# Expert pass in another order, with the whole weights loaded in two steps and the last waits moved to SyncE

## The reference

```python
def reference(x, ...):
    xn = _layernorm(x)
    return x + attention(xn) + ffn(xn)

def attention(x):                       # causal linear attention with a gate
    xn = _layer_norm(x, ln_g, ln_b)
    q, k, v = split(xn @ qkv_w + qkv_b)
    k = elu(k * sigmoid(xn @ gate_w + gate_b)) + 1
    q = elu(q) + 1
    num = (tril(q @ k.T)) @ v
    den = sum(q * cumsum(k)) + 1e-6
    return num / den

def ffn(x):                             # eight experts, two per token
    gates = sinkhorn((x @ router_w.T + router_b) / temp)
    topk_vals, topk_idx = top_k(gates, 2)
    g, p = relu(x @ wg[e]), x @ wp[e]   # 128 -> 256
    all_out[e] = (g * p) @ wo[e]        # 256 -> 128
    return x + sum(all_out[topk_idx] * topk_gates)
```

## Time and profile before

| | us |
|---|---|
| median of 3 runs | 374.01 (373.85 to 376.59) |
| profiled execution, its own time | 375.94 |
| its span, first to last instruction | 373.90 |
| TensorE busy | 335.1 |
| GpSimd busy | 267.3 |
| VectorE busy | 268.1 |
| ScalarE busy | 235.6 |
| mean granted clock of TensorE | 0.978 |

### The profile page before, as it was taken

One profiled execution on the slowest core, in us unless ns is written; L12 is line 12 of the kernel. 1 busy time (PEld: TensorE's weight loads), 2 busy tenths in 40 slices (PEclk: granted clock), 3 DMA queues, 4 the chain that ended last, 5 costly groups with the idle time before them and its releaser, 6 DMA issues.

```text
span 373.9 us, 8933 instructions
## 1 busy us (share of the span) xinstructions
PE 335.1 (90%) x2584; PEld 304.9 (82%) x2584; DVE 268.1 (72%) x735; ACT 235.6 (63%) x442; POOL 267.3 (71%) x363
## 2 busy tenths in 40 slices
PE   0799899888999999988779999999999999999980
PEld 0789568656888888868779999999989999999980
DVE  3998889989888888785625667666666667666650
ACT  2689753225766766756525787777767777776540
POOL 3686999955777766657627767777777777777772
PEclk9999999989999999999969999999999999999996
DMA  6999999997434423248988887554565565564110
GB/s 179 285 327 334 337 332 276 319 258 231 145 108 142 144 100 118 84 127 232 310 270 259 254 228 200 176 161 129 154 188 158 163 163 164 142 185 114 58 35 0
DMA packets 64285, 70.97 MB, mean 190 GB/s; under 512 B 6098, under 2 KB 59102, under 8 KB 64240
## 3 DMA queue, kind: packets, MB, share of 16 engines
q1 hardware_dynamic: 54112, 48.70, 48.2%
q0 software_dynamic: 8672, 21.19, 15.7%
q10 hardware_dynamic: 1456, 0.53, 0.7%
HBM read 28.54 MB, written 43.04 MB: 191 GB/s over the span
## 4 chain that ended last, share of the span: by engine, by line
PE 69%; DVE 15%; DMA 6%; issue 4%; POOL 3%; ACT 2%; SPq 0%; POOLq 0%; ACTq 0%; DVEq 0%
PE psum L1712 16%; PE psum L1697 7%; PE psum L1699 7%; PE psum L1698 7%; PE psum L1687 5%; PE psum L1585 4%; PE psum L1521 4%; PE psum L1673 4%; PE psum L1414 3%; DVE stats L887 3%; DMA rows<-by_lower 2%; DMA rows<-in_L_attn_x 2%; POOL out L598 2%; PE psum L1467 2%; PE psum L1468 2%
## 5 line engine op out<-in xcount | busy, mean ns | idle before, releaser
L576 POOL DMA_INDIRECT by_lower<-rows,slot_u x64 | 63.9, 999 | 29.9 <-issue 18.5
L598 POOL DMA_INDIRECT out<-rows x70 | 68.8, 983 | 21.5 <-issue 16.2
L1712 PE MATMUL psum<-w_expert,hT 128*128 x560 | 77.5, 278 | 0.8 <-DVE hT L1347 0.5
L1697 PE MATMUL psum<-xT_high,w_now 128*128 128x256 f32 x232 | 70.4, 303 | 1.9 <-DVE xT_low L1338 1.2
L587 POOL DMA_INDIRECT by_upper<-rows x58 | 57.1, 985 | 20.3 <-issue 12.0
L1712 PEld LDWEIGHTS psum<-w_expert,hT 128*128 128x128 f32 x560 | 69.8, 193 | 1.5 <-issue 1.1
L799 ACT ACTIVATE w_now<-w_split 128x1024 fp32r x58 | 61.4, 1059 | 13.4 <-PE psum L1699 12.8
L1698 PE MATMUL psum<-xT_low,w_now 128*128 128x256 f32 x232 | 65.4, 282 | 0.0
L1699 PE MATMUL psum<-xT_high,w_now 128*128 128x256 f32 x232 | 65.3, 282 | 0.0
L1351 DVE TENSOR_TENSOR hT<-relu,psum 128x512 f32<-128x512 f32 x58 | 39.9, 687 | 33.7 <-ACT relu L818 17.1
L818 ACT ACTIVATE relu<-psum 128x512 f32<-128x512 f32 x58 | 34.6, 597 | 20.4 <-PE psum L1699 20.4
(11 more groups left out here) (271 smaller groups left out, 705.7 us busy)
## 6 DMA issues: line engine op xcount, KB each, us to landing
by_lower<-blank SPq DMA_DIRECT2D x1, 10140.0 KB, 35.3
by_upper<-blank SPq DMA_DIRECT2D x1, 10062.0 KB, 71.3
rows<-by_upper SPq DMA_DIRECT2D x29, 258.0 KB, 2.9
rows<-by_lower SPq DMA_DIRECT2D x23, 260.0 KB, 3.4
rows<-in_L_attn_x SPq DMA_DIRECT2D x8, 512.0 KB, 9.1
lead_row<-by_lower SPq DMA_DIRECT2D x6, 260.0 KB, 2.8
rows<-by_lower SPq DMA_DIRECT2D x12, 130.0 KB, 4.4
rows<-by_upper SPq DMA_DIRECT2D x12, 129.0 KB, 2.3
```

Of the source, the lines that this page charges most:

```text
L576: pool.indirect_dma_start(by_lower, bass.IndirectOffsetOnAxis(ap=slot_u[:, t:t + 1], axis=0), rows[:, t, :], None)\
L598: pool.indirect_dma_start(out_rows, bass.IndirectOffsetOnAxis(ap=row(n)[:, k, TOKEN:TOKEN + 1].bitcast(U32), axis=0), row(n)[:, k, BASE], ...
L1697: pe.matmul(target, high, x_high, start=True, stop=False)
L1712: last = pe.matmul(psum[:, 4 + n % 2, k * D:(k + 1) * D], hT[:, n % 3, f, k * P:(k + 1) * P], weights, start=(f == 0), stop=(f == FB - 1))
```

## The change

It has four parts. `FRONT` = 18 takes the place of `LEAD` as the number of long entries ahead of the twelve short ones, so the first pass is eighteen long, twelve short and eleven long entries; the lead buffers stay six. The floor of `need_first` becomes 18. The weights of `w_whole` are issued in two steps, the first ahead of the load of entry 10, the second ahead of entry 12, and the last expert's weights ahead of entry 20; the places where ScalarE and VectorE split them move along. And the waits for the last 18 `row_out` semaphores go from GpSimd to SyncE.

```diff
+    FRONT = 18
...
-    FIRST_PASS = [*range(LEAD), *range(PAIRS, NE), *range(LEAD, PAIRS)]
+    FIRST_PASS = [*range(FRONT), *range(PAIRS, NE), *range(FRONT, PAIRS)]
...
             for n in range(LEAD):
                 load_row(n, by_lower, ROW)
-            sp.wait_ge(o_chunk, G)
-            sp.dma_start(w_whole[:, :, 0:FF], wg.rearrange("e p f -> p e f")).then_inc(whole_loaded, 16)
-            sp.dma_start(w_whole[:, :, FF:2 * FF], wp.rearrange("e p f -> p e f")).then_inc(whole_loaded, 16)
             for n in range(LEAD, NE):
                 if n == LEAD + 4:
+                    sp.wait_ge(o_chunk, G)
+                    sp.dma_start(w_whole[:, :, 0:FF], wg.rearrange("e p f -> p e f")).then_inc(whole_loaded, 16)
+                if n == LEAD + 6:
+                    sp.dma_start(w_whole[:, :, FF:2 * FF], wp.rearrange("e p f -> p e f")).then_inc(whole_loaded, 16)
+                if n == FRONT + 2:
                     load_expert(E - 1)
                 load_row(n, by_lower, ROW)
             for n in range(NE, 2 * NE):
                 load_row(n, by_upper, ROW_UP)
+            for n in range(2 * NE - NB, 2 * NE):
+                sp.wait_ge(row_out[n % NB], gone_after(n))
...
-            for n in range(2 * NE - NB, 2 * NE):
-                pool.wait_ge(row_out[n % NB], gone_after(n))
...
-                    if a == 0 and i == LEAD + 14:
+                    if a == 0 and i == FRONT + 12:
                         round_expert(E - 1)
...
-                        if n + 4 == LEAD:
+                        if n + 4 == FRONT:
                             act.wait_ge(whole_loaded, 32)
...
-                step(dve.tensor_scalar(need_first[:], need[:], pair_end[:, 0:1], float(LEAD), ALU.add, ALU.max))
+                step(dve.tensor_scalar(need_first[:], need[:], pair_end[:, 0:1], float(FRONT), ALU.add, ALU.max))
...
-                    if a == 0 and i == LEAD + 15:
+                    if a == 0 and i == FRONT + 13:
                         divide_expert(E - 1)
```

## The result

| | before | after |
|---|---|---|
| median, timed in the same rounds | 376.55 (6 runs) | 370.01 (6 runs) |
| ratio after / before | | 0.984 (0.981 to 0.988) |
| profiled execution, its own time | 375.94 | 368.30 |
| its span | 373.90 | 365.50 |
| last scatter into by_lower to last scatter to out ("the stage") | 190.35 | 184.63 |

The changed kernel is 6.5 us faster by the medians and 5.9 by the ratio. Three of the six runs of before are those whose median was 374.01 ahead of the change. The forecast was 8.1 us faster and 365.9; the measured 370.0 lies above the range (364.4 to 369.0).

A forecast was written before the change was run, and what follows sets the result against it. It took TensorE to bound the kernel, with GpSimd almost as late; 6.8 us from the hole before entry 6 and 1.3 at the end, 8.1 off 374.01, gave 365.9 us, range 364.4 to 369.0.

The forecast's parts named there:

- The hole before entry 6: Start of the expert stage: TensorE's idling and slow clock, with entry 6's load behind the weights, cost 6.8 us, all regained.
- The landing of entry 6: After the last by_lower scatter: 3.4 us for the scatter, 3.4 for the load, landed at 183.0, 1.7 us early.
- No loss at entries 10 and 12: First pass, row loads behind the moved weights: between 6 us early and 2.8 us late, loss taken as nothing.
- rival B: First pass: entry 12 up to 2.8 us late, or GpSimd idling more; about 1.5 us back, 367.4; chance 0.17.
- The second pass and its later floor: Second pass: first load at about 248, 11 us later than before, at no cost, with 16 us of cover.
- GpSimd follows: Expert stage: GpSimd runs through the first pass to 268.9 and is 1.8 us early for the second.
- The end: End of program: with SyncE waiting for the last landings, GpSimd's DRAIN starts earlier; 1.3 us gained, between 0 and 2.3.
- rival A: End of program: GpSimd's DRAIN waits for the landing on its own, so only 6.8 us are won, 367.2; chance 0.20.
- The sum: Whole kernel: 6.8 us from the hole before entry 6 plus 1.3 at the end, 8.1 us in all.
- The absolute number: Whole kernel: 8.1 us taken from the median of 374.01, giving 365.9 us.

The follow-up runs named there:

- t_before: The kernel before, unchanged, run against itself to show the noise; ratio 0.996 (0.993 to 1.000).
- s_after: The changed kernel, unchanged, run once more beside other runs; 370.1 us, 0.983 of before.
- t_poolwaits: The changed kernel with the last eighteen waits back on GpSimd instead of SyncE; 0.987 of before.
- s_by_expert: The changed kernel with the whole weights in sixteen transfers of 128 KB, two ahead of each load of entries 8 to 15; 368.4 us, 0.981 of before.
- s_second_at_16: The changed kernel with the second half of the whole weights issued ahead of entry 16 instead of entry 12; 369.5 us, 0.983 of before.

## Why the prediction was right or wrong

Two terms of the forecast failed: the base of the sum, 374.01, which was 2.5 us too low, and the loss at entry 12, which was put at nothing and was 1.1 us. The mechanism at entry 6 and that at the end were right.

- **The hole before entry 6.** Right in cause and size: 6.8 us were put on it, and the stage without any hole is 6.5 to 6.8 us shorter than before's first profile (190.35 - 183.6 to 183.9). In the later profile of before (t_before) the stage was 191.6. TensorE lost 0.7 us more there (turn of entry 5 to turn of entry 8 in 14.5 us against 13.7) after much the same hole, 5.00 us: its granted clock was still 0.71 from 194 to 196, where it was 1.00 in the first profile. And GpSimd, waiting 1.63 and 1.45 us for landings in the short entries, never idled again before the second pass, so it was the later of the two. So the hole costs 6.5 to 8.0, and GpSimd's reserve in the old order was small. The stretch of t_before:

```profile
194.00:196.00 2.00, 2.00 (x15) 2.00 (x15) 0.81 (x3) 0.00 (x0) 0.72 (x1) 0.71 0.45 113
```

- **The landing of entry 6.** Mis-sized. The forecast had 3.4 for the scatter and 3.4 for the load, and 1.7 us to spare. The scatter took 3.82. The trace of after has no landing for entry 6's own load, but the next one took 4.6; with that it landed at 183.25 for a turn at 183.35, so nothing was to spare. In s_after it was 0.54 late. Of the lead loads the forecast had only 2.8; in later profiles their median was 3.4 to 4.3, in either order.
- **No loss at entries 10 and 12.** This is the step of the argument that failed; entry 10 was in time, entry 12 was not. The text set 283 KB per us (6 us early) against 168 (2.8 late) and took no loss. The measured rate from the issue of entry 6's load to the landing of entry 12's is 3868 KB / (199.61 - 178.65) = 185 KB per us, and 175 in s_after, close to the slow bound, which was itself a measured row. The fast one was no row at all: 0.92 us was SyncE's pace of issue for four loads of short entries, 130 KB each, and the text gave it 260 KB. The hole before entry 12 was 1.1 us in the profile of after, 1.5 and 0.2 in two others (s_after, t_poolwaits). It was named as rival B with a chance of 0.17; it should have been the forecast. The rule of the Trainium skill (DMA: Bandwidth & Descriptors, section "Queues, rings and completion order"), that descriptors are consumed in ring order on each DMA engine, stood beside it and pointed to this. The runs agree: in after the load behind the second 1024 KB took 12.3 us, in s_by_expert those with 256 KB of weights between them 4.3 to 5.9.
- **The second pass and its later floor.** Right: its first load went out at 246.4 (248 forecast), and TensorE did not idle on a row there.
- **GpSimd follows.** Right in that it was not the later one, and in part by luck. It did not run through the short entries: it lost 0.7 and 1.0 us there beyond its pause of 0.30, waiting for VectorE's rows. Of the 1.8 us forecast for the start of the second pass 0.9 were left (1.16 less the pause), and that with TensorE a hole later than forecast.
- **The end.** Right, 1.3 us of the span, by the mechanism that was taken: the DRAIN is 4.98 us of GpSimd's own time from the end of its last instruction. The DRAIN's row read 7.64 us, and a DRAIN that had grown was what the prediction had put down as the sign of rival A; that sign was badly chosen, since an earlier start alone lengthens it. In the other profiles with SyncE waiting it starts 0.2 to 2.3 us before the last scatter, reads 6.2 to 8.2 us, and ends 4.98 after that scatter's instruction each time. Rival A is out: the end did shrink.
- **The sum.** 8.1 forecast. In the stage and at the end 5.7 + 1.3 = 7.0; the missing 1.1 is the second hole. In device time 5.9 to 6.5: the rest, 0.5 to 1.1 us, is about what the new order has more around its span (2.8 to 4.2 us in the six executions of after, where the sum kept the 2.04 of before). The sum had no term for that, and its cause stays open.
- **The absolute number.** The larger part of the miss of 4.1 us is the base. The 8.1 were taken from 374.01, the median of three runs. In the rounds of after the median of before was 376.55, and 376.3 to 377.5 in the three other groups. The profiled run's own 375.94, which the text set aside, was the better base: it would have given 367.8. So 2.5 us of the miss are the base and 1.6 the gain. The base alone put the result outside: with 376.55 the forecast would have been 368.5 and the same range 367.0 to 371.5. Without the hole before entry 12 but with the old base it would not have been met either: s_second_at_16 took 369.5 us.

## What to carry to other kernels

When a stall comes from a small transfer behind a large one on the same queue, moving the large one back only moves the stall, unless its new neighbours can wait for all of its bytes at the slowest rate that the trace shows; cutting it into pieces and placing them between the loads removes it. Take the supply rate from a stretch where the DMA engines are full, not from the pace of issue. An engine with a long DRAIN at the end should have nothing in front of it that another engine can wait for; and a gain of 2% should be taken from a base of more than three runs.

## What the runs showed of the hardware

- GpSimd's DRAIN at the end is done 4.98 us after the end of its last DMA instruction where it starts before that, and takes 4.98 us from its own start where it comes behind the waits, in every profile. Those of TensorE, VectorE and ScalarE took 0.39 to 0.60 us, SyncE's 7 ns where it has the waits.
- Issuing a row load on SyncE took 2.79 us instead of 0.37 for the load of entry 12, the first behind both transfers of 1024 KB; it took 2.83 for the first load behind both in s_second_at_16, and with pieces of 128 KB no row load's issue took over 0.75. Both transfers ahead are not enough for it: in before, where entry 6's load went out 3.1 us behind them with no other row load in between, it took 0.36. What makes it long is not shown. This is the view of line 424 in after, from 186.5 to 188:

```profile
L424 SPq DMA_DIRECT2D rows<-by_lower x1: 2792/2792/2792, 187.3 to 187.3; - x1
```

- An idle stretch of 4.85 to 5.97 us brought the granted clock to 0.50; idling of 1.06 us (after) and 1.48 us (s_after) left it at 1.00, and the turns that followed were 2.5 us apart again.
- The same program took 376 us in three groups and about 446 in two, with stalls of TensorE that the trace gives no releaser for, and one chip had both. In those two groups the gain of the change could not be measured at all. What causes them stays open.
